# Rotary attention in a decoder layer: q and k projected dimension-major, halves swapped by copies within SBUF, the context turned by the host, the table of units reordered

## The reference

```python
x = x + attn(_layernorm(x), Wq, Wk, Wv, Wo)               # 16 heads of 64, rotary q and k
x = x + xattn(_layernorm(x), ctx, mask, Wq, Wkv, Wout, bout)  # 16 heads, q rows masked
x = x + moe(_layernorm(x), Wg, We, be)                    # softmax gate, best 2 of 8 experts

def _rope(x, cos, sin):                                   # x: ..., T, 64
    xe, xo = x[..., 0::2], x[..., 1::2]
    re, ro = xe * cos - xo * sin, xe * sin + xo * cos
```

## Time and profile before

| | |
|---|---|
| median of 3 runs | 4115.7 us |
| profiled execution | 4114.02 us, span 4112.2 us |
| PE busy | 3739.3 us, 91% |
| DVE, ACT, POOL busy | 2348.8 us (57%), 2205.0 (54%), 2190.4 (53%) |
| granted clock of PE, mean | 0.98 |
| DMA | 46.42 MB, mean 11 GB/s |

### The profile page before, as it was taken

How to read it: one execution, slowest core, us unless ns; L and a number is a source line. 1 busy time by engine, 2 the same in 40 slices (tenths; PEclk the granted TensorE clock), 3 DMA queues, 4 the chain that set the end, 5 groups by cost and what they waited for, 6 DMA issues and landing times.

```text
span 4112.2 us, 88113 instructions
## 1 busy us (share of the span) xinstructions
PE 3739.3 (91%) x30272; PEld 3121.3 (76%) x30272; DVE 2348.8 (57%) x6089; ACT 2205.0 (54%) x6442; POOL 2190.4 (53%) x2664
## 2 busy tenths in 40 slices
PE   4899999999999999999999999999999999999997
PEld 3777777777777777777777777777777777777776
DVE  5555555555555555555555655555555555555554
ACT  4555555555555555555555555555555555555563
POOL 3555565555565455554555655556545555555562
PEclk9999999999999999999999999999999999999999
DMA  3000000000000000000000000000000000000000
GB/s 110 4 11 10 8 8 11 7 10 11 6 11 7 11 10 11 6 11 7 10 11 6 11 7 11 10 8 8 9 8 10 11 6 11 7 10 10 6 10 6
DMA packets 44329, 46.42 MB, mean 11 GB/s; under 512 B 8008, under 2 KB 40784, under 8 KB 43856
## 3 DMA queue, kind: packets, MB, share of 16 engines
q1 hardware_dynamic: 43136, 39.89, 3.2%
q10 hardware_dynamic: 720, 0.09, 0.0%
HBM read 31.58 MB, written 8.39 MB: 10 GB/s over the span
## 4 chain that ended last, share of the span: by engine, by line
PE 77%; DVE 11%; issue 6%; ACT 4%; DMA 1%; DVEq 0%; POOL 0%; ACTq 0%; POOLq 0%
PE unit_ps L435 18%; PE oT_ps L575 12%; PE pT_ps L558 10%; PE score_ps L542 9%; PE unit_ps L457 9%; PE unit_ps L447 8%; PE wo_ps L599 7%; PE unit_ps L466 3%; ACT probs L692 2%; DVE probs L815 2%; DVE x L889 2%; DVE rope_a L827 2%; ACT pT L681 1%; DVE rope_b L827 1%; DVE k_lo L821 1%
## 5 line engine op out<-in xcount | busy, mean ns | idle before, releaser
L990 POOL TENSOR_TENSOR inv_sum<-row_sum,minus_one 128x2 f32<-128x2 f32 x1024 | 713.1, 696 | 1248.6 <-ACT probs L692 1245.5
L994 POOL TENSOR_TENSOR probs<-probs,inv_sum 128x512 f32<-128x512 f32 x1024 | 1067.3, 1042 | 80.4
L815 DVE TENSOR_SCALAR_CACHE_REDUCE probs<-score_ps,mask_add 128x256 f32<-128x256 f32 x1024 | 447.5, 481 | 452.1 <-PE score_ps L542 281.6
L681 ACT ACTIVATE pT<-pT_ps 128x512 f32<-128x512 f32 x1024 | 614.6, 600 | 137.1 <-PE pT_ps L558 137.1
L692 ACT ACTIVATE probs<-score_ps,neg_max 128x256 f32<-128x256 f32 x1024 | 480.4, 484 | 356.5 <-DVE neg_max L804 356.5
L692 ACT ACTIVATE probs<-probs,neg_max 128x256 f32<-128x256 f32 x1024 | 509.5, 501 | 288.4 <-DVE probs L815 288.3
L558 PE MATMUL pT_ps<-ident,probs 128*128 128x128 f32 x4096 | 639.1, 282 | 1.9 <-POOL probs L994 1.9
L558 PEld LDWEIGHTS pT_ps<-ident,probs 128*128 128x128 f32 x4096 | 454.8, 142 | 209.9 <-issue 174.1
L575 PE MATMUL oT_ps<-pT,v_sb 128*64 128x256 f32 x4096 | 573.6, 402 | 34.2 <-ACT pT L681 34.2
L435 PE MATMUL unit_ps<-w_hi,xs_lo 128*128 128x256 f32 x1536 | 466.1, 303 | 65.4 <-DVE rope_b L827 62.6
L804 DVE TENSOR_REDUCE neg_max<-score_ps 128x2 f32<-128x512 f32 x512 | 329.6, 686 | 284.8 <-PE score_ps L542 281.1
(11 more groups left out here) (112 smaller groups left out, 8539.7 us busy)
## 6 DMA issues: line engine op xcount, KB each, us to landing
x_in<-dram_x SPq DMA_DIRECT2D x32, 256.0 KB, 2.7
xn<-dram_ctx SPq DMA_DIRECT2D x32, 256.0 KB, 2.7
layer_out<-x SPq DMA_DIRECT2D x32, 256.0 KB, 2.2
rope_b<-dram_bout SPq DMA_DIRECT2D x32, 128.0 KB, 3.0
probs<-dram_ckv SPq DMA_DIRECT2D x6, 256.0 KB, 4.0
probs<-dram_we SPq DMA_DIRECT2D x4, 256.0 KB, 3.8
pT<-dram_we SPq DMA_DIRECT2D x4, 256.0 KB, 4.0
probs<-dram_sq SPq DMA_DIRECT2D x3, 256.0 KB, 3.5
```

The source lines that it names most:

```text
L681: nc.scalar.activation(flat(pT[:, s % 2, :, :]), pT_ps[s % 2][:], ACT.Copy).then_inc(pT_ready.sem, 1)
L815: last = nc.vector.tensor_scalar(probs[:, s % P_BUFS, t, :], ps[:, t * T:(t + 1) * T], mask_add[:, t:t + 1], None, ALU.subtract, ALU.min, ...
L990: nc.gpsimd.tensor_tensor(inv, row_sum[:, h % STATS, :], minus_one[:], ALU.pow).then_inc(inv_ready.sem, 1)
L994: nc.gpsimd.tensor_tensor(weights, weights, inv.unsqueeze(2).to_broadcast([P, NT, T]), ALU.mult).then_inc(probs_ready.sem, 1)
```

## The change

Q and K of the first attention are made by `dim_major` like those of the second. ScalarE copies the raw product out of PSUM into one of two tiles `rope` (partition: dimension, even dimensions first in each head, then odd). SP copies `rope` to `swap` in four copies of 32 partitions (64 KB each), so that each half of a head stands at the other half's partitions. Two slots after the unit (`TURN`) VectorE multiplies `rope` by `cos_sb`, POOL multiplies `swap` by `sin_sb` (its sign in the host's table) and adds it to `rope`; three slots after (`SPLIT`) ScalarE and VectorE split `rope` from SBUF. The turns QT, KT of groups 0 to 3 are gone. The context comes from the host with its dimensions first, is loaded into `xn` in SP's slot 4, and is split from there in slot 6; CT is gone. The table of units, some places in `AT`, and the place of five output projections (ahead of the slot's units) are new. LATE now holds for each kind on ScalarE too.

```diff
-NOW, LATE, SOON = range(3)
+NOW, LATE = range(2)
 UNITS = {
-    0: [("QT", 1, 0, NOW), ("KP", 1, 0, NOW)],
-    1: [("V", 1, 0, LATE)],
-    2: [("KT", 1, 0, SOON), ("QP", 2, 0, LATE)],
-    3: [],
-    4: [("KP", 2, 0, NOW), ("QT", 2, 0, LATE)],
-    5: [("V", 2, 0, LATE)],
-    6: [("KT", 2, 0, SOON), ("QP", 3, 0, NOW)],
-    7: [],
-    8: [("KP", 3, 0, NOW), ("QT", 3, 0, LATE)],
-    9: [("V", 3, 0, LATE), ("L3", 0, -1, LATE)],
-    10: [("LG", 0, -1, NOW), ("KT", 3, 0, NOW)],
-    11: [("EX", 0, -1, LATE)],
-    12: [("CT", 0, 0, NOW)],
-    13: [("EX", 1, -1, NOW), ("KT", 4, 0, NOW)],
-    14: [],
-    15: [("KT", 5, 0, LATE)],
-    16: [("EX", 2, -1, NOW)],
-    17: [("EX", 3, -1, NOW), ("GT", 0, -1, LATE)],
-    18: [("EX", 4, -1, NOW), ("V", 4, 0, NOW), ("V", 5, 0, NOW)],
-    19: [("EX", 5, -1, NOW), ("L2", 0, 0, NOW), ("QT", 4, 0, NOW), ("EX", 6, -1, NOW)],
-    20: [("EX", 7, -1, NOW)],
-    21: [("BI", 0, -1, NOW), ("QT", 5, 0, LATE)],
-    22: [],
-    23: [],
-    24: [("QT", 6, 0, LATE)],
-    25: [("KT", 6, 0, LATE)],
-    26: [],
-    27: [("KT", 7, 0, SOON)],
-    28: [("V", 6, 0, NOW), ("QT", 7, 0, LATE)],
-    29: [("L1", 0, 1, SOON)],
-    30: [("QP", 0, 1, NOW), ("V", 7, 0, NOW)],
-    31: [],
-    32: [("QT", 0, 1, SOON), ("KP", 0, 1, NOW)],
-    33: [("V", 0, 1, NOW)],
-    34: [("QP", 1, 1, NOW), ("KT", 0, 1, NOW)],
+    0: [],
+    1: [("Q", 2, 0, LATE)],
+    2: [],
+    3: [("K", 2, 0, NOW)],
+    4: [("V", 1, 0, NOW), ("Q", 3, 0, NOW)],
+    5: [("L3", 0, -1, NOW)],
+    6: [("V", 2, 0, NOW)],
+    7: [("LG", 0, -1, NOW)],
+    8: [("K", 3, 0, LATE), ("EX", 0, -1, LATE)],
+    9: [],
+    10: [("EX", 1, -1, LATE), ("EX", 2, -1, LATE)],
+    11: [("V", 3, 0, LATE)],
+    12: [],
+    13: [("K", 4, 0, NOW)],
+    14: [("EX", 3, -1, LATE)],
+    15: [],
+    16: [],
+    17: [("EX", 4, -1, NOW)],
+    18: [("EX", 5, -1, NOW), ("K", 5, 0, NOW), ("V", 4, 0, LATE), ("EX", 6, -1, NOW), ("L2", 0, 0, LATE)],
+    19: [("Q", 4, 0, NOW), ("EX", 7, -1, NOW), ("GT", 0, -1, NOW)],
+    20: [("Q", 5, 0, NOW), ("BI", 0, -1, LATE)],
+    21: [],
+    22: [("Q", 6, 0, NOW)],
+    23: [("V", 5, 0, NOW)],
+    24: [],
+    25: [("K", 6, 0, NOW)],
+    26: [("Q", 7, 0, LATE), ("K", 7, 0, LATE)],
+    27: [("L1", 0, 1, NOW)],
+    28: [],
+    29: [("Q", 0, 1, NOW)],
+    30: [("V", 6, 0, NOW)],
+    31: [("K", 0, 1, LATE)],
+    32: [],
+    33: [("Q", 1, 1, LATE)],
+    34: [("V", 7, 0, LATE), ("V", 0, 1, LATE), ("K", 1, 1, LATE)],
...
+def rotated(s, behind):
+    turn, at = divmod(s - behind, SLOTS)
+    return [(kind, g, off + turn) for kind, g, off, _ in UNITS[at] if kind in ("Q", "K") and g < NG]
+def order_of(kind, g):
+    return 2 * g + (kind == "K")
...
-    "gate weights": 11,
-    "gate table": 11,
-    "mask": 19,
-    "statistics 2": [18, 2],
+    "gate weights": 8,
+    "gate table": 8,
+    "context": 6,
+    "mask": 1,
+    "statistics 2": [18, 0],
     "norm 2": [18, 2],
     "x to x1": 23,
-    "statistics 1": 27,
-    "norm 1": 28,
+    "statistics 1": 25,
+    "norm 1": 26,
-    "projection first": [],
+    "projection first": [7, 11, 27, 31, 35],
...
-        rope_a = sb("rope_a", [P, NT, GW])
-        rope_b = sb("rope_b", [P, NT, GW])
-        gatesT, bout_sb = rope_b[0:E, 0, 0:T], rope_b[:, 1, 0:D]
+        rope = sb("rope", [P, 2, NC, T])
+        swap = sb("swap", [P, NC, T])
+        gatesT, bout_sb = swap[0:E, 0, 0:T], swap[:, 1, 0:D]
...
+                return raw_ready, order_of(kind, g) + 1
+            return {"V": (v_ready, g + 1), "Q": (q_ready, g + 1), "K": (k_ready, g + 1),
...
+            def swap_halves(b, kind, g, off):
+                n = order_of(kind, g)
+                sp.wait_ge(roped.sem, roped.at(b, off, n))
+                sp.wait_ge(raw_ready.sem, raw_ready.at(b, off, n + 1))
+                for quarter in range(4):
+                    to, of = quarter * HALF, (quarter ^ 1) * HALF
+                    sp.dma_start(swap[to:to + HALF, :, :], rope[of:of + HALF, n % 2, :, :]) \
+                        .then_inc(swapped.sem, 16)
             def body(b):
                 for s in range(SLOTS):
+                    if s == AT["context"] - 2 and exists(b, 0):
+                        sp.wait_ge(xs_turned.sem, xs_turned.at(b, 0, 1))
+                        if exists(b, -1):
+                            sp.wait_ge(xf_turned.sem, xf_turned.at(b, -1, 1))
+                        sp.dma_start(xn[:], ctx_d[b].rearrange("(c p) t -> p c t", p=P)) \
+                            .then_inc(ctx_loaded.sem, 16)
                     for kind, g, off, _ in UNITS[s]:
...
+                        if kind in ("Q", "K") and g < NG and exists(b, off):
+                            swap_halves(b, kind, g, off)
+                        if kind == "K" and g == NG and exists(b, 0):
...
+                    pe.wait_ge(xs_ready.sem, xs_ready.at(b, off, 1 if g < NG else 2))
+                    dim_major(ps, xs_hi, xs_lo, 0 if g < NG else 4, g % NG).then_inc(q_projected.sem, 1)
+                elif kind == "K" and g < NG:
                     pe.wait_ge(xs_ready.sem, xs_ready.at(b, off, 1))
+                    dim_major(ps, xs_hi, xs_lo, 1, g).then_inc(k_projected.sem, 1)
+                elif kind == "K":
+                    pe.wait_ge(ctx_ready.sem, ctx_ready.at(b, off, 1))
+                    dim_major(ps, ct_hi, ct_lo, 5, g - NG).then_inc(k_projected.sem, 1)
...
-                    nc.scalar.activation(flat(k_hi[:, g % 2, :, :]), ps, ACT.Copy).then_inc(k_hi_ready.sem, 1)
-                elif kind == "CT":
-                    act.wait_ge(ctx_turned.sem, ctx_turned.at(b, off, 1))
-                    nc.scalar.activation(flat(ct_hi[:]), ps, ACT.Copy).then_inc(ctx_hi_ready.sem, 1)
+                elif kind in ("Q", "K") and g < NG:
+                    n = order_of(kind, g)
+                    projected, ready = (q_projected, q_ready) if kind == "Q" else (k_projected, k_ready)
...
+                    act.wait_ge(ready.sem, ready.at(b, off if g else off - 1, g if g else NG))
+                    act.wait_ge(projected.sem, projected.at(b, off, g + 1))
+                    nc.scalar.activation(flat(rope[:, n % 2, :, :]), ps, ACT.Copy).then_inc(raw_ready.sem, 1)
+                elif kind in ("Q", "K"):
+                    projected = q_projected if kind == "Q" else k_projected
+                    act.wait_ge(projected.sem, projected.at(b, off, g + 1))
+                    high_part(b, ps, kind, g, off)
...
+            def high_part(b, src, kind, g, off):
+                before = g - 2 if g >= 2 else g + 2 * NG - 2
+                act.wait_ge(scored.sem, scored.at(b, off if g >= 2 else off - 1, HG * before + HG))
+                if kind == "Q":
+                    nc.scalar.activation(flat(q_both[:, g % 2, 0:2, :]), src, ACT.Copy,
+                                         scale=q_scale(g)).then_inc(q_hi_ready.sem, 1)
+                else:
+                    nc.scalar.activation(flat(k_hi[:, g % 2, :, :]), src, ACT.Copy).then_inc(k_hi_ready.sem, 1)
+            def split(b, kind, g, off):
+                n = order_of(kind, g)
+                act.wait_ge(roped.sem, roped.at(b, off, n + 1))
+                high_part(b, flat(rope[:, n % 2, :, :]), kind, g, off)
...
+                    if s == AT["context"] and exists(b, 0):
+                        act.wait_ge(k_projected.sem, k_projected.at(b, -1, 2 * NG))
+                        act.wait_ge(v_projected.sem, v_projected.at(b, -1, 2 * NG))
+                        act.wait_ge(ctx_loaded.sem, ctx_loaded.at(b, 0, 1))
+                        nc.scalar.activation(flat(ct_hi[:]), flat(xn[:]), ACT.Copy).then_inc(ctx_hi_ready.sem, 1)
+                    for kind, g, off in rotated(s, SPLIT):
+                        if exists(b, off):
+                            split(b, kind, g, off)
...
+            def cosines(b, kind, g, off):
+                n = order_of(kind, g)
+                dve.wait_ge(swapped.sem, swapped.at(b, off, n + 1))
+                nc.vector.tensor_tensor(rope[:, n % 2, :, :], rope[:, n % 2, :, :],
+                                        cos_sb[:].unsqueeze(1).to_broadcast([P, NC, T]),
+                                        ALU.mult).then_inc(cos_done.sem, 1)
+            def unit(b, ps, kind, g, off):
+                if kind in ("Q", "K") and g >= NG:
...
+                    for kind, g, off in rotated(s, TURN):
+                        if exists(b, off):
+                            cosines(b, kind, g, off)
+                    for kind, g, off in rotated(s, SPLIT):
+                        if exists(b, off):
+                            split(b, flat(rope[:, order_of(kind, g) % 2, :, :]), kind, g, off)
+                    if s == AT["context"] and exists(b, 0):
+                        dve.wait_ge(ctx_hi_ready.sem, ctx_hi_ready.at(b, 0, 1))
+                        low_part(ct_lo[:], flat(xn[:]), ct_hi[:]).then_inc(ctx_ready.sem, 1)
...
+                    for kind, g, off in rotated(s, TURN):
```

(41 more changed lines are left out.)

96 lines of the change are left out of this document (23 added, 73 removed).

## The result

Before, 4112.1 us (median of 5 runs, 4105.8 to 4116.8); changed, 4146.5 us (4144.7 to 4163.7): a ratio of 1.0096, 95% interval 1.0071 to 1.0121. The change makes the kernel about 1% slower; 3970 us was forecast, so 176 us are to be found.

What follows compares the result with a forecast made beforehand. PE's in-order queue was taken as the bound, busy 3739.3 of 4112.2 us. Per element 4.05 + 1.95 + 1.7 - 3.2 = 4.5 us, 144 in all: 4114 - 144 = 3970 us, own range 3900 to 4030, overall range 3850 to 4120.

Steps and rivals of the forecast that it cites:

- Turns removed: On PE's queue: nine turns (QT, KT, CT) at 0.45 us each disappear, gaining 4.05 us an element.
- `rope_b`'s waits: On PE: two waits per element for the second rotary product to free a unit bank disappear, gaining 1.95 us.
- Refill: On PE after the drain: Q5, BI, Q6 and V5 fill the gaps around slots 20 to 23, gaining 1.7 us an element.
- The rotation: Raw copy to `roped` through ScalarE, SP and POOL: 6.2 us each, bounds 5.6 to 7.8, eight an element.
- Rival D: Slower: six serial rotations, Q1 to K3, become the bound from about 8.5 us a rotation; 4160 us, chance 15%.
- New waits: Waits of PE caused by the eight added rotations, at four places: 3.2 us an element lost, bounds 0 and 10.
- (a): Slot 0 onward: K1's copies wait for Q1's rotation, so POOL scales heads 0 and 1 late; 1.6 us.
- (d): Near slot 8's scores: Q3's rotation, held behind K2's and the context's load, ends late; 0.4 us.
- A rule beside a row: 17 two-SBUF-input VectorE instructions an element: the sum assumed no blocking by POOL, following row L962, against the skill's rule.
- Rival C: VectorE and POOL shut each other out: 2.2 us an element reach PE, 4040 us, chance 13%.
- Clock: PE after the gate's 12 small matmuls: a 4 us stretch at granted 0.57, partly 1.2 GHz, carried unchanged.
- rival B: No new waits, since slack of three probability tiles absorbs them: 3868 us, chance 15%.

Runs made afterwards that it cites:

- e1: Changed kernel with the four SBUF copies of each rotation left out, so the result is incomplete: 3879.9 us, ratio 0.9450 to the kernel before.
- e7: Changed kernel with one piece of the old unit order back, around slots 18 to 24 behind the drain: 4266.9 us, ratio 1.0384 to the kernel before.
- the doses: Changed kernel with two of each rotation's four SBUF copies left out, or each copy cut in two: 4022.0 and 4672.5 us.
- e6: Changed kernel with each of a rotation's four SBUF copies cut in two, same bytes, eight issues: 4672.5 us, ratio 1.1381 to the kernel before.
- e9: Changed kernel with VectorE's cosine product replaced by a tiny memset, so the rotation is incomplete: 4096.7 us, ratio 0.9966 to the kernel before.

## Why the prediction was wrong, by its own steps

**Turns removed, 4.05 us an element.** Consistent with the runs, but not isolated. In e1 PE is busy 182 us less than before, where I had said 175; that closeness is in part luck, since e1 also has 94 us less at the lower clock than before (76 against 170). At the table's 0.37 us per us that is an estimated 35 us, and about 147 are left for the turns.

**`rope_b`'s waits, 1.95.** Right: no such releaser is left.

**Refill, 1.7.** The right mechanism, mis-sized: 3.8 (e7). I counted the three waits of the timeline, but not the stretch at the lower clock behind them, 1.3 us of pair (24,25) before and 1.6 in e7, nor what slots 14 to 21 gain by having EX7 earlier.

**The rotation, 6.2 us: the step that failed.** The copies of one that stands alone were nearly right: from the end of the raw copy to the start of the sine product 4.0 us (K3, mean of the table's elements), where I had 1.5 + 2.3; landing is 2.0. But the sine product is 1.60 in the mean and the sum 1.36, not 1.04 each, and K3's sum waits 0.6 us for the cosine product besides, so that one alone takes 7.2 us to `roped`, not 6.2. And few stand alone: over all eight the mean is 9.0, of which 1.2 is waiting for the rotation before. SP holds the next rotation's copies back until `roped`, and K1's then cost up to 4.7 us (2085.93 to 2090.64) in front of POOL. My upper bound of 7.8 doesn't come out of its own rows: 1.5 + 3.0 + 1.04 + 1.48 + 0.3 is 7.3. Rival D said "from about 8.5 us a rotation" and 4160 us: 15% for what came (4146). Its mechanism, rotations that queue, is borne out by the doses; its arithmetic, a chain saturated from Q1 to K3, isn't (its sum gives 4159): the pairs (4,5) and (10,11) lost nothing, and K2's copies had landed 3.5 us before POOL took them, since POOL stood at `rstd` for VectorE until 2107.72 (the line above) and had a head to scale after it.

**New waits, 3.2.** The places were named, the price wasn't. (a) was said to be 1.6 us for heads 0 and 1; it is the pair (2,3), 6.2 us more than before, 5.5 more than without copies. (d), at 0.4, is 1 us in pair (6,7) against e1, through K2's split and not Q3's, and another 1.8 in (8,9), in whose 7.9 us 4.5 are at the lower clock. I let every rotation start when it was ready and looked at its end; POOL's and VectorE's queues are blocked from the moment the wait reaches their front. The signs I had named came half way: PE's waits for POOL and ScalarE at turns and scores, to grow by 100 us in my forecast and by over 250 in D, rose from 3 us to 221 (180.9 and 39.7), and POOL's wait for `swapped` passes 3 us at 29 of 256 rotations.

**A rule beside a row.** I went by L962 with its 686 ns; it fell. The same sum, now on `swap` (L1005), takes up to 827, and both engines' instructions stretch (ns min/median/max):

```profile
L866 DVE SCALAR_TENSOR_TENSOR q_both<-rope,q_both x128: 691/694/1785, 63.1 to 4023.7; 128x512 fp32r<-128x512 f32 x128
...
L1046 POOL TENSOR_TENSOR swap<-swap,sin_sb x256: 1271/1736/1799, 59.3 to 4032.3; 128x512 f32<-128x512 f32 x128
```

Max less min is 1.1 us on VectorE, one POOL product of 1.04. In e6, where both products wait for the last copy, all 256 cosine products take 0.69 to 0.70 us and no sine product less than 1.76. The rule of the Trainium skill, "SBUF — State Buffer", section "Who interferes with whom", that a two-input SBUF instruction of VectorE and a GpSimd instruction that reads SBUF exclude each other, agrees with these traces. A row of 32 instructions at one fixed place in the schedule had said nothing about 17 at others: `ct_lo` takes 1754 to 1768 ns each of its 32 times. Rival C's mechanism is real; the part of it that was priced, the eight cosine products, is 50 us with their own work (e9). Its price was also mis-added: a quarter of 10.1 us is 2.5 an element and not 2.2.

**Clock: "I carry it unchanged".** The second failure. 170 us at the lower clock became 413, and PE's busy time is 126 us above e1's. My own rows pointed at it: the earlier trace rows showed matmuls at half clock behind the gate's 12 small ones, and I added waits without asking what stands behind them.

In sum, by my own terms: with the refill as measured the gains are 4.05 + 1.95 + 3.8 = 9.8 us an element, and the kernel lost 1.0, so the term "new waits" stands for 10.8 and not 3.2 (an estimate, from the terms above and the measured time). The copies, with what lock they bring about, make 8.3 of it: 267 us, of which 141 are PE's idle time and 126 its busy time at the same matmuls, which I put down to the clock. I had put all new waits at 102 us and the clock at 0. That e1's 3880 lies near rival B's 3868, the price with no new waits, is luck: PE still waits 100.6 us for POOL there, and the refill gives 2.1 us an element more than B has.
